# A whitening and AFNO block on one core: the MLP in plain fp32 with its second layer turned, LN1's weight applied at an eviction, its bias at one frequency, and both put into the residual on GpSimd

## The reference, cut to what matters

```
x = whiten(x)                       # (16,56,56,64): covariance over all tokens, Cholesky, gamma, beta
residual = x
h = layer_norm(x) * n1_g + n1_b     # per token, over 64 channels
f = rfft2(h)                        # over the 56x56 grid
f = two complex layers of 8x8 blocks (relu between), softshrink(0.01)
h = irfft2(f) + h + residual
residual = h
h = layer_norm(h) * n2_g + n2_b
h = gelu(h @ mw1 + mb1)             # 64 -> 256, erf gelu
out = h @ mw2 + mb2 + residual      # 256 -> 64
```

## Time and profile before

| what | value |
|---|---|
| median of 3 runs | 1024.01 us |
| profiled execution, its span | 1024.67 us, 1022.9 us |
| TensorE matmul busy | 88% of the span |
| TensorE weight load busy | 76% |
| VectorE, ScalarE, GpSimd busy | 70%, 49%, 26% |
| mean granted clock of TensorE | 0.919 of full |

### The profile page before, as it was taken

One profiled execution on the slowest core, in us unless ns is written; L12 is line 12 of the kernel. 1 busy time (PEld: TensorE's weight loads), 2 busy tenths in 40 slices (PEclk: granted clock), 3 DMA queues, 4 the chain that ended last, 5 costly groups with the idle time before them and its releaser, 6 DMA issues.

```text
span 1022.9 us, 18505 instructions
## 1 busy us (share of the span) xinstructions
PE 899.1 (88%) x6391; PEld 780.4 (76%) x6391; DVE 717.3 (70%) x2063; ACT 505.4 (49%) x947; POOL 261.5 (26%) x107
## 2 busy tenths in 40 slices
PE   5889972887999988998999899998999999799687
PEld 5886552785789768976997699878987997599465
DVE  4456779179967876787678767776778788743762
ACT  0002001563676565756575657555755655675333
POOL 2000001333433133213321342234223422430110
PEclk8995565897999999999899989999999999999799
DMA  9940102002000210011001200020000000000001
GB/s 253 264 114 18 46 1 63 1 1 63 1 20 19 61 31 18 18 41 50 18 19 33 58 9 27 18 73 9 27 19 11 20 19 29 1 28 22 16 28 37
DMA packets 9956, 40.97 MB, mean 40 GB/s; under 512 B 1232, under 2 KB 1232, under 8 KB 8208
## 3 DMA queue, kind: packets, MB, share of 16 engines
q1 hardware_dynamic: 9888, 40.19, 14.2%
HBM read 27.34 MB, written 12.85 MB: 39 GB/s over the span
## 4 chain that ended last, share of the span: by engine, by line
PE 55%; DVE 24%; issue 10%; DMA 5%; ACT 4%; DVEq 0%; SPq 0%; ACTq 0%
PE psum L1054 15%; PE psum L1039 8%; PE psum L992 8%; DMA n<-x_dram 5%; DVE stats L543 5%; PE psum L973 4%; PE psum L922 3%; PE psum L861 3%; PE psum L934 3%; PE psum L944 3%; PE psum L1013 3%; DVE o_g L294 2%; ACT o_g L1146 2%; PE psum L909 2%; DVE n L584 2%
## 5 line engine op out<-in xcount | busy, mean ns | idle before, releaser
L1178 ACT ACTIVATE hid<-psum,hbias 128x448 f32<-128x448 f32 x224 | 136.4, 634 | 151.4 <-PE psum L1039 150.5
L1054 PEld LDWEIGHTS psum<-prm,hid 128*112 128x112 f32 x1792 | 184.1, 180 | 8.5 <-ACT hid L1178 4.7
L1054 PE MATMUL psum<-prm,hid 128*112 128x96 f32 x1792 | 188.4, 264 | 2.2 <-ACT hid L1178 2.2
L364 POOL TENSOR_TENSOR hbuf<-hbuf,prm 112x1792 f32<-112x1792 f32 x15 | 51.6, 3440 | 333.8 <-DVE hbuf L617 333.8
L666 DVE TENSOR_TENSOR n2T<-psum,n2T 64x448 fp32r<-64x448 f32 x112 | 69.7, 622 | 89.0 <-ACT n2T L1170 87.6
L1039 PE MATMUL psum<-n2T,mw1h 128*128 128x448 f32 x224 | 103.4, 461 | 25.2 <-DVE n2T L666 11.9
L392 POOL TENSOR_TENSOR p_y<-over,under 116x512 f32<-116x512 f32 x64 | 77.6, 1214 | 158.1 <-ACT under L1196 158.1
L992 PE MATMUL psum<-cst,p_y 116*128 116x224 f32 (+1 forms) x480 | 100.6, 352 | 3.0 <-POOL p_y L392 3.0
L992 PEld LDWEIGHTS psum<-cst,p_y 116*128 116x128 f32 (+1 forms) x480 | 89.0, 191 | 5.9 <-POOL p_y L392 3.2
L1039 PE MATMUL psum<-n2T,mw1l 128*128 128x448 f32 x224 | 84.3, 376 | 0.0
L371 POOL TENSOR_TENSOR rbuf<-hbuf,ybuf 112x3584 f32<-112x3584 f32 x8 | 62.9, 7865 | 70.0 <-DVE fbuf L703 63.9
(11 more groups left out here) (114 smaller groups left out, 1662.4 us busy)
## 6 DMA issues: line engine op xcount, KB each, us to landing
xin<-x_dram SPq DMA_DIRECT2D x9, 1568.0 KB, 9.0
out_dram<-oslice SPq DMA_DIRECT2D x56, 224.0 KB, 2.2
ybuf<-x_dram SPq DMA_DIRECT2D x2, 1568.0 KB, 20.1
fbuf<-x_dram SPq DMA_DIRECT2D x2, 1568.0 KB, 23.5
n<-x_dram SPq DMA_DIRECT2D x2, 1568.0 KB, 26.6
xin<-x_dram SPq DMA_DIRECT2D x4, 392.0 KB, 6.2
prm<-params_dram SPq DMA_DIRECT2D x1, 899.5 KB, 28.7
cst<-consts_dram SPq DMA_DIRECT2D x1, 716.0 KB, 20.5
```

The lines of the kernel that those rows point to most:

```text
L1054: last = nc.tensor.matmul(t[0:ROWS, at:at + 96], hid[:, m, w % 2, (w // 2) * ROWS:(w // 2 + 1) * ROWS], pp("mw2")[:, 128 * m + zeros:128 * ...
L1178: nc.scalar.activation(hid[:, q % 2, q // 2, :], ring_c[k % RING_C][:, 0:4 * ROWS], ACT.Gelu, bias=hbias[:, q % 2:q % 2 + 1]).then_inc(c_a ...
```

## The change

1. MLP. The fp32r split goes: `n2T` is one fp32 tile [128, 448] (channels of even columns in partitions 0 to 63, of odd ones in 64 to 127), evicted by one ScalarE copy. `mlp_in` does a hidden half m with two fp32 matmuls of 64 partitions each, v = 0 and v = 1, into two banks. `mlp_out` is turned: `mw2` is the weight (128 x 64), `hid` the moving data (448 columns), v = 0 into PSUM partitions 0 to 63 and v = 1 into 64 to 127. ScalarE evicts this with mb2 as bias (`ev_mlp_t`), four transposes (`turn_out`) bring it into rows. `mlp_out` and `turn_out` of slice s stand in slice s+1, those of slice 6 beside `inv_h` 4 to 7.
2. LN2 doesn't subtract the mean: it is taken out of `mw1s` once, with a matmul and one instruction. `mean_rstd` of LN2 has 15 links in place of 17.
3. LN1's weight is the scale of the column transform's eviction (`ev_dft_w`: two ScalarE instructions a tile in place of one); its bias is added at frequency zero (two small ones more, after a wait). VectorE's L617 goes.
4. GpSimd: the two biases go. The residual is three instructions over 3584 elements: y + b1, h * g1 in place after `dft_h` has read h, and the sum.
5. Softshrink: x - clamp(x). VectorE clamps after its eviction, ScalarE's two Relus go.
6. Banks: ring B has 3 banks and ring C 3; layer 1 may use C's banks too. All of n2, mlp and out use bank 2 of C. `transpose_n` of slice 0 now waits for all evictions of layer 1.

```diff
-RING_A, RING_B, RING_C = 2, 4, 2
+RING_A, RING_B, RING_C = 2, 3, 3
+B_BANK[L1:L1 + 8] = [1, 2, 3, 4, 0, 5, 1, 2]
+C_BANK = [what[3] if what[0] == "hid" else 2 for what in C_ORDER]
                 def residual(i):
+                    pool.wait_ge(n1_ready, 2 * i + 2)
                     if not isinstance(i, int) or i > 0:
                         pool.wait_ge(b_dve, i * B_DVE)
-                    pool.wait_ge(h_ready, i * 2 + 1)
-                    nc.gpsimd.tensor_tensor(r4, h_tok, y4, ALU.add).then_inc(r_ready, 1)
+                    nc.gpsimd.tensor_tensor(r3, y3, row("b1", W), ALU.add).then_inc(r_begun, 1)
+                    pool.wait_ge(pe_b, i * B_CHUNKS + S2)
+                    nc.gpsimd.tensor_tensor(h4, h4, pp("g1", ROWS)..., ALU.mult).then_inc(h_gain, 1)
+                    pool.wait_ge(h_gain, i + 1)
+                    pool.wait_ge(r_begun, i + 1)
+                    nc.gpsimd.tensor_tensor(r4, r4, h_tok, ALU.add).then_inc(r_ready, 1)
-                def bias_h(i):
-                def bias_f(i):
...
                 def ln2(i):
                     mean_rstd(i, 1)
                     for k in range(2):
-                        subtract_mean(fbuf, n2, 1, k)
-                        multiply_rstd(n2, i, 1, k).then_inc(n2_ready, 1)
+                        multiply_rstd(i, k)
...
                 def ev_layer_2(i, half, ks):
-                            dve.wait_ge(shrunk, i * 8 + c - L2_BUFS + 1)
+                            dve.wait_ge(y_ready, i * 8 + c - L2_BUFS + 1)
...
+                        nc.vector.tensor_scalar(clamped[:, c % L2_BUFS, 0:n], layer2[:, c % L2_BUFS, 0:n], LAM, -LAM,
+                                                ALU.min, ALU.max).then_inc(shrunk, 1)
...
+                def mlp_in(i, s, m):
+                    if m == 0:
+                        pe.wait_ge(c_act, i * C_ACT + C_ACT_DONE["n2", s])
+                    for v in range(2):
+                        t = free_c(i, C_AT["hid", s, m, v])
+                        nc.tensor.matmul(t[:, 0:4 * ROWS], mw1s[C * v:C * v + C, HH * m:HH * m + HH],
+                                         n2T[C * v:C * v + C, :], start=True, stop=True).then_inc(pe_c, 1)
+                def mlp_out(i, s):
+                    t = free_c(i, C_AT["mlp", s])
+                    pe.wait_ge(c_act, i * C_ACT + C_ACT_DONE["hid", s, 1, 1])
+                    for m in range(2):
+                        for v in range(2):
+                            last = nc.tensor.matmul(t[C * v:C * v + C, 0:4 * ROWS], pp("mw2")[:, C * m:C * m + C],
+                                                    hid[:, s % 2, m, v, :], start=(m == 0), stop=(m == 1))
+                    last.then_inc(pe_c, 1)
                 def mlp(i, s, fill):
+                    mlp_in(i, s, 0)
+                    fill(0)
+                    fill(1)
+                    mlp_in(i, s, 1)
+                    if s > 0:
+                        mlp_out(i, s - 1)
                     fill(2)
                     if s < SLICES - 1:
                         transpose_n(i, s + 1)
                     fill(3)
+                    if s > 0:
+                        turn_out(i, s - 1)
...
+                    if behind:
+                        mlp_out(i - 1, SLICES - 1)
+                    inv_h(i, 4)
+                    inv_h(i, 5)
+                    if behind:
+                        turn_out(i - 1, SLICES - 1)
+                    inv_h(i, 6)
+                    inv_h(i, 7)
...
+                        for h in range(2):
+                            last = nc.scalar.activation(p_v[:, :, h, 4 * k:4 * k + n, :], t[:, :, h], ACT.Identity,
+                                                        scale=pp("g1c")[:, h:h + 1])
```

More of the change, by code:

```diff
@@ L713, in step, with slice_ @@
                 def step(i, ahead, behind):
-                    def slice_(s, before, after):
-                        before()
-                        if behind and s < SLICES - 1:
-                            ev_rest(i - 1, s + 1)
-                        after()
-                        if behind:
-                            ev_mlp(i - 1, s)
+                    def slice_(s, e0, e1, e2, e3):
+                        e0()
+                        e1()
+                        e2()
+                        if behind and s > 0:
+                            ev_mlp(i - 1, s - 1)
+                        e3()
                     def next_(what, *args):
@@ L848, in covariance @@
                     last.then_inc(s_pe, 1)
+                    nc.tensor.matmul(mwm_ps, pilot_w[0:C, :], mw1s[0:C, :], start=True, stop=True).then_inc(s_pe, 1)
                 def factor():
@@ L1098, in step @@
                     slice_(6, lambda j: (turn(i, [4 + j]), inv_h(i, j)))
-                    for k in range(4, 8):
-                        inv_h(i, k)
+                    if behind:
+                        mlp_out(i - 1, SLICES - 1)
+                    inv_h(i, 4)
+                    inv_h(i, 5)
+                    if behind:
+                        turn_out(i - 1, SLICES - 1)
+                    inv_h(i, 6)
+                    inv_h(i, 7)
                 covariance()
@@ L1116, in _ @@
                     mlp(PAIRS - 1, s, lambda j: None)
+                mlp_out(PAIRS - 1, SLICES - 1)
+                turn_out(PAIRS - 1, SLICES - 1)
             @block.scalar
@@ L1201, in slice_ @@
                         if behind:
-                            gelu(i - 1, s, fill)
+                            mlp(i - 1, s, fill)
                         else:
@@ L1235, in step @@
                     slice_(6, lambda j: ev_turn(i, [4 + j]))
+                    if behind:
+                        ev_mlp_t(i - 1, SLICES - 1)
                 act.wait_ge(s_dve, DV_MEAN)
@@ L1251, in _ @@
                 for s in range(SLICES):
-                    gelu(PAIRS - 1, s, lambda j: None)
+                    mlp(PAIRS - 1, s, lambda j: None)
+                ev_mlp_t(PAIRS - 1, SLICES - 1)
 GR = C + KR
```

401 lines of the change are left out of this document (180 added, 221 removed).

## The result

The changed kernel takes 1058.11 us (median of 4 runs, 1055.80 to 1059.21) against 1024.22 us for the kernel before on the same chip: ratio 1.0349, 95% interval 1.0313 to 1.0385. It is slower by 34 us, where I had forecast 14. The profiled execution took 1057.11 us with a span of 1055.2.

What follows compares the result with a forecast made beforehand. TensorE's stream was taken as the bound, except where it waits. Steps 1 to 7 +26.7, before step 0 -8.6, step 0 -4, last MLP 0: +14 on 1024.67, given as 1038 us, range 1004 to 1064.

Steps and rivals of the forecast that it cites:

- last MLP: The MLP at the kernel's end: 7.3 us a slice against 7.04 before, 0 together, between -6 and +4.
- The hold: Head of a step: GpSimd's three residual instructions, 22.4 us, keep VectorE's two-input LN2 chain waiting until 2.9 us after them.
- Rival (a): Head of a step: VectorE slips through between GpSimd's instructions, 10 us less a step, about 968 us; chance 0.12.
- Rival (c): MLP: the column halves run one behind another, 1.2 us more in each of 56 slices, about 1105 us; chance 0.12.
- Rival (b): Head of a step: lock with cheaper GpSimd terms, 19 us in place of 22.4, 1012 to 1026 us; chance 0.17.
- Result 58.6 with the transitions: Slices 1 to 6 of a step: 58.6 us against 60.35 before, from a cheaper MLP, mlp_out of slice 6 and waits.
- A wait put at nothing: Ahead of slice 1: the forecast sum there has 0.4 us and no wait for ScalarE's copy of n2.
- The lower clock: Head of a step: after 10 us without work TensorE runs whitening and what follows at 1.7 us in place of 0.9 each.
- My 46.6: Head of a step: slice 1 starts 46.6 us after TensorE starts inv_h 4, against 42.9 before, so +3.7.
- Clamps: VectorE in slices 1 and 2: taken at 0.4 us each, costed at nothing; 2.4 us a step if the cover goes.
- `ev_dft_w` at nothing: ScalarE's column-transform eviction, 0.8 us a tile beside TensorE's 0.9: costs nothing, at most 0.5.
- The wait at `mlp_out` of slice 6: TensorE waits 0.8 us there because bank 2 is still read by ev_mlp.

Runs made afterwards that it cites:

- e1_defer: The changed kernel with GpSimd's last two residual instructions put off until the normalised tile of the pair before is complete: 990.07 us, ratio 0.9678 to the kernel before.
- e5_extra1: The kernel before the change, with one more GpSimd instruction of two SBUF inputs ahead of the residual sum: 1058.37 us, ratio 1.0331.
- e5_extra2: The kernel before the change, with two more GpSimd instructions of two SBUF inputs ahead of the residual sum: 1105.14 us, ratio 1.0787.
- e2_short: The changed kernel with the residual's second and third GpSimd instructions left out: 991.82 us, ratio 0.971 to the kernel before.
- e4_parts: e1_defer with the two halves of mlp_out issued apart, one more half-array stretch per slice: 1002.04 us, ratio 0.9808 to the kernel before.
- e8_warm: The changed kernel with eight unread matmuls in TensorE's empty stretch behind layer 1: 1044.67 us, ratio 1.0194 to the kernel before.

## Why the direction was right and the size wrong

The stretches, forecast and measured, in us against before (profiled execution against profiled execution):

| stretch | forecast | measured |
|---|---|---|
| up to T0 of step 1 | -12.6 | -16.5 |
| step 1 | +7.4 | +8.2 |
| steps 2 to 5 | +6 | +17.8 |
| step 6 | +7.8 | +9.1 |
| step 7 | +5.5 | +12.1 |
| last MLP | 0 | +1.6 |
| sum | +14 | +32.3 |

**The hold: right.** I had put GpSimd's three instructions at 22.4 us from T0+4.8 to T0+27.3; they run from T0+5.0 to T0+27.0 (21.96 with gaps). The chain ended at T0+30.2 as forecast (482.07), the last layer-1 eviction at T0+37.85 (38.1). That this, and not the MLP, makes the kernel slower is shown by `e1_defer` from one side and by `e5_extra1` and `e5_extra2` from the other. By the Trainium skill, SBUF — State Buffer, section Who interferes with whom, the pair of ports is locked for the whole instruction; the links of 7.91, 6.26 and 7.82 us agree.

**Rival (a), VectorE slips through: fell.** At a border the held link ends and at most one more passes. Its time was wrong too: without the two instructions the kernel takes 990 and not 968. In `e2_short` the chain ends at T0+22.5 (456.52 from 434.02), 1.5 later than in the rival; seven times 1.5 is not quite half of the 24 between 968 and this kernel's 992, and the rest lies in the terms below, which this kernel has too (slice 1 at T0+39.5 in step 3 where the rival has 36, and slices 1 to 6 in 60.2).

**Rival (c), the column halves one behind another: fell.** Eight `mlp_out` records take 1.65 us from the first start to the next operation. **Rival (b)**: its instructions cost 22.0, not 19.

Split at the start of slice 1, the seven steps are off as follows (us from T0 to slice 1, then slices 1 to 6):

| step | forecast | measured |
|---|---|---|
| 1 | 46.6 + 58.6 | 45.8 + 60.25 |
| 2 to 5, mean | 46.6 + 58.6 | 47.9 + 60.25 |
| 6 | 46.6 + 55.9 | 46.6 + 57.2 |
| 7 | 41.6 + 55.9 | 44.4 + 59.7 |

Of the 18 us between forecast and result, slices 1 to 6 hold 13.4 and the way to slice 1 holds 7.1; the last MLP adds 1.6, and 3.9 go off again ahead of step 1. The chain of the forecast was right further than its end: in step 3 the first hidden matmuls were over at T0+42.51 (494.40), and I had 42.5.

**The step that failed: what a stretch of half-array tiles costs its neighbours.** "Result 58.6 with the transitions" holds 57.65 from the terms written there (60.35 - 4.5 + 1.8 + 0.8 + 1.1 - 1.9) and 0.95 for going into and out of half-array tiles, in six slices. The matmuls of slices 1 to 6 in step 3 that don't belong to the MLP took 29.92 before and 32.34 after: 2.4 where I had 0.95. The MLP itself, with its waits, came out as worked out (27.9; by my terms 27.7). So the slices took 60.25, a tenth of a microsecond less than before, in place of 1.8 less; over seven steps the 1.5 us too little are some 10 of the 18 us. TensorE's time in step 3 by operation, summed from the trace from the start of each record to the start of the next:

| operation | before | after |
|---|---|---|
| MLP (hidden, second layer, turn_out) | 36.06 | 31.09 |
| layer 1, with the wait behind it | 8.52 | 15.47 |
| whitening | 9.56 | 10.81 |
| layer_2, inv_w, turn | 21.69 | 24.20 |
| inv_h | 6.73 | 7.33 |
| transposes of x and n2 | 7.77 | 6.88 |

The MLP saved 4.97, 0.71 a slice, as forecast (0.75). But its neighbours grew by 2.5 and 0.6 (0.3 of it a wait): the last full-array matmul ahead of a half-array stretch and the first one behind it take 0.203 us to the next start in place of 0.109 (medians over all slices), and the last pair in a stretch 0.466 in place of 0.38. That is 0.28 a stretch, and `e4_parts` shows nearly that size by adding one: 0.19. Twelve stretches at that price are 2.3 of the 2.4 us. I had put 0.25 into a pair of 1.0; with its neighbours it is 1.14. Cheaper than forecast was `mlp_out` (1.65 for 1.8), dearer `turn_out` (0.48 for 0.4). The Trainium skill has the rule without a price (TensorEngine Tiling (Array Packing), Key Properties: changing the mode drains TensorE); the 0.203 agrees with it.

**A wait put at nothing: ScalarE's copy of n2 ahead of slice 1.** From the transposes of n2 to slice 1 I had 0.4; it is 1.25 in step 3 (499.18 to 500.43), with 0.70 of TensorE without work. In the old order 3.08 us of second-layer matmuls stood between the two; the change moved these into slice 1. The wait of 0.70 (0.62 in steps 6 and 7) stands in every step of every kernel here that has the new MLP, at either clock. Seven times 0.8 are some 6 of the 18 us. That moving other work there would win them was not tried.

**The lower clock: right in size for six steps, wrong for step 7.** My 46.6 had the transposes, whitening tile 3 and the first hidden group at the lower clock, some 2 us a step over full clock. In step 3 it lasted one group longer (16 whitening records in 2.86 us to the next start, where I had 1.8), in steps 4 and 6 not so long (1.93). By `e8_warm` the lower clock cost steps 1 to 6 10.6 us together, where I had about 12. Step 7 is another matter. I had taken off seven whitening tiles of 0.9 there; but in the other steps three of them stand ahead of the transposes of n2, which come when VectorE is done: leaving these out brought the transposes forward by 1.7 us (T0+36.3 against 38.0), not 2.7. And the lower clock lasted into slice 1, whose whole first fill ran at 1.2 GHz,

```profile
926.26 3.73 PE L933 MATMUL psum<-w2s,o_g 128*116 128x128 f32 x16
```

3.73 in place of 2.00. Step 7 took 104.1 and not 97.5, and `e8_warm` gives 5.1 of that back.

**Smaller terms.** Clamps, 0.43 us each (median), at nothing in steps 1 to 7: the traces agree. `ev_dft_w` at nothing: layer 1 runs without a wait. The wait at `mlp_out` of slice 6: 0.8 forecast, 0.96 in slice 6's place. The last MLP has 7.5 us a slice, 7.3 forecast. The sign "slices 1 to 6 shorter than before" held by 0.1 us only. Before step 0 8.8 us were saved (8.6 forecast), in step 0 7.7 (4 forecast); why step 0 gained 3.7 more stays open.

## What to carry to other kernels

Before a long GpSimd instruction with SBUF inputs is placed, look at which of VectorE's instructions have two SBUF inputs then: a chain of small dependent ones pays the whole length of each GpSimd instruction. The same work one wait later cost nothing, and turned +3.5% into -3.2%. Half-array matmuls are to be priced with what their neighbours lose: 0.2 to 0.3 us for each stretch here, which took back nearly all that the shorter MLP had saved in slices 1 to 6. A wait of TensorE is to be priced with what runs behind it at the lower clock (here up to five groups, 4.1 us behind a wait of 9.5). And when work is moved, look at which wait it had covered.

## What the runs showed of the hardware

- A real loop on VectorE brought a pause that the profile calls issue: 5.23 and 2.78 us in step 3 of `e1_defer` with the loop, none with the loop written out, and the statistics then run as one group of 49 in 6.29 us. It is worth nothing where another wait covers it (1.0319 against 1.0349).
- Two column halves of the array run side by side: the second record of a pair starts 7 ns behind the first.
